# A VectorE addition between two DMAs of sums, one product with ones behind the out projection, and a new order at both ends

## The reference

```python
h = _layernorm(x)
mod = jax.nn.silu(time) @ mod_w + mod_b
shift, scale, gate = jnp.split(mod, 3, axis=-1)
h = h * (scale + 1.0) + shift
qkv = (h @ w_qkv).reshape(B, T, 3, H, e).transpose(2, 0, 3, 1, 4)
q, k, v = (qkv[0], qkv[1], qkv[2])
q = _apply_rope(_layernorm(q, q_norm_w), position)   # rotates the first 16 of 32
k = _apply_rope(_layernorm(k, k_norm_w), position)   # the other 16 pass unchanged
scores = jnp.einsum('bhqe,bhke->bhqk', q, k) / jnp.sqrt(jnp.asarray(e, q.dtype))
attn = jax.nn.softmax(scores, axis=-1)
o = jnp.einsum('bhqk,bhke->bhqe', attn, v)
o = o.transpose(0, 2, 1, 3).reshape(B, T, D)
return x + o @ w_out * gate
```

## Time and profile before

| | us |
|---|---|
| median of 3 runs | 1816.01 (1814.66 to 1819.8) |
| profiled execution | 1818.37 |
| its span, first to last instruction | 1816.5 |
| TensorE products busy | 1691.9 (93%) |
| VectorE busy | 1248.4 (69%) |
| ScalarE busy | 1024.5 (56%) |
| GpSimd busy | 721.3 (40%) |

### The profile page before, as it was taken

One profiled execution on the slowest core, in us unless ns is written; L12 is line 12 of the kernel. 1 busy time (PEld: TensorE's weight loads), 2 busy tenths in 40 slices (PEclk: granted clock), 3 DMA queues, 4 the chain that ended last, 5 costly groups with the idle time before them and its releaser, 6 DMA issues.

```text
span 1816.5 us, 32141 instructions
## 1 busy us (share of the span) xinstructions
PE 1691.9 (93%) x12326; PEld 987.8 (54%) x12326; DVE 1248.4 (69%) x1595; ACT 1024.5 (56%) x1544; POOL 721.3 (40%) x708
## 2 busy tenths in 40 slices
PE   5878899999999999999999999999999999998777
PEld 3544455555555555555555555555555555554334
DVE  8666666777777676767777776767777676765443
ACT  3335655655565566556555655665566556655442
POOL 2533244344334434443443444344434434443121
PEclk9879999999999999999999999999999999999888
DMA  6024354545545454655555464555545554544454
GB/s 216 13 47 99 83 133 105 126 107 128 117 105 135 111 132 96 134 117 107 126 119 126 99 137 108 112 121 125 125 102 131 113 115 111 128 99 96 108 116 116
DMA packets 55446, 206.43 MB, mean 114 GB/s; under 512 B 6640, under 2 KB 6640, under 8 KB 38912
## 3 DMA queue, kind: packets, MB, share of 16 engines
q0 software_dynamic: 18432, 134.23, 38.7%
q1 hardware_dynamic: 36864, 70.14, 11.3%
HBM read 53.25 MB, written 16.88 MB: 39 GB/s over the span
## 4 chain that ended last, share of the span: by engine, by line
PE 67%; DVE 21%; issue 6%; ACT 4%; DMA 2%; SPq 0%; POOL 0%; DVEq 0%; ACTq 0%; POOLq 0%
PE SA L393 10%; PE Y L320 10%; DVE cst L954 8%; PE Y L307 8%; PE MB L421 7%; PE O L412 7%; PE SM L363 6%; PE Y L310 6%; PE Y L314 6%; DVE qk_lo L943 4%; ACT probs L716 4%; DVE xin L921 3%; PE SA L397 3%; DVE bn L876 2%; PE SA L297 1%
## 5 line engine op out<-in xcount | busy, mean ns | idle before, releaser
L954 DVE TENSOR_REDUCE cst<-SM 128x2 fp32r<-128x1024 f32 x256 | 313.5, 1225 | 329.1 <-PE MB L363 329.1
L1174 POOL DMA_DIRECT2D probs<-probs x128 | 111.6, 872 | 777.6 <-ACT probs L718 748.8
L716 ACT ACTIVATE probs<-SM 128x1024 f32<-128x1024 f32 x256 | 262.0, 1023 | 260.4 <-PE SM L397 257.8
L954 DVE TENSOR_REDUCE cst<-MB 128x2 fp32r<-128x1024 f32 x256 | 311.4, 1216 | 0.0
L412 PE MATMUL O<-probs,vals 128*32 128x512 f32 x2048 | 277.1, 614 | 0.0
L718 ACT ACTIVATE probs<-SA 128x1024 f32<-128x1024 f32 x256 | 261.0, 1019 | 0.0
L623 ACT ACTIVATE rows<-Y 128x512 f32<-128x512 f32 x123 | 73.5, 598 | 281.5 <-PE Y L314 281.5
L307 PE MATMUL Y<-wqkv_hi,hT_hi 128*128 128x512 f32 x724 | 218.3, 424 | 2.8 <-ACT hT_hi L592 2.8
L310 PE MATMUL Y<-wqkv_hi,hT_lo 128*128 128x512 f32 x724 | 197.8, 396 | 6.2 <-DVE hT_lo L937 6.2
L363 PEld LDWEIGHTS SM<-qk_hi 32*128 32x128 f32 x512 | 50.0, 184 | 270.5 <-issue 80.0
L314 PE MATMUL Y<-wqkv_lo,hT_hi 128*128 128x512 f32 x724 | 195.9, 393 | 0.0
(11 more groups left out here) (197 smaller groups left out, 3466.2 us busy)
## 6 DMA issues: line engine op xcount, KB each, us to landing
probs<-probs POOLq DMA_DIRECT2D x128, 1024.0 KB, 7.7
xin<-in_x_dram SPq DMA_DIRECT2D x62, 256.0 KB, 6.9
xres<-in_x_dram SPq DMA_DIRECT2D x60, 256.0 KB, 2.6
out_dram<-xres SPq DMA_DIRECT2D x60, 256.0 KB, 3.8
shift_scale<-mod_rows SPq DMA_DIRECT2D x15, 512.0 KB, 5.9
gate<-mod_rows SPq DMA_DIRECT2D x16, 256.0 KB, 5.3
probs<-in_L_cond_w_qkv_dram SPq DMA_DIRECT2D x2, 1024.0 KB, 11.3
rows<-in_L_cond_mod_w_dram SPq DMA_DIRECT2D x2, 1024.0 KB, 11.2
```

What stands on the lines that cost most here:

```text
L716: act.activation(probs[:, a, 2:4, :], SM[:], ACT.Exp).then_inc(s_exp, 1)
L954: dve.tensor_reduce(heads[:, 2 * half:2 * half + 2, 0], bank[:], AX.X, ALU.max, negate=True).then_inc(max_out, 1)
```

## The change

**Sums over keys.** VectorE's `add_pair(s)` adds buffer 0 onto buffer 2, after the first DMA has landed and TensorE has weighed t = 2. The second DMA adds buffer 1 onto buffer 2 after that. One product with ones of buffer 2 is left; it stands in the next step behind the out projection, ahead of the third scores by key. ScalarE takes the logarithm directly from the bank, behind `guess_roots`; the copy and `add_sums` are gone. `key_exponentials(s, 0)` waits for `add_pair(s - 1)` in place of the product with ones.

**Rotation.** The second operation of `rotate` covers only the 16 rotated columns of each head. The weights of q's and k's norm for the other 16 are applied as a factor per partition (`pass_w`) in `high_qk` and `low_qk`.

**Order of VectorE.** In a step, x's statistics stand behind the maxima of t = 0, `normalize_x` at the step's end, `add_pair` ahead of the maxima of t = 3. **Order of GpSimd.** `output_low` stands ahead of the second DMA. **Order of ScalarE.** `output_high` follows the exponentials of t = 2 in every step.

**Head.** The weights of the modulation are loaded first; the statistics of the first six tiles are taken in three parts (1, 3 and 2 tiles); tiles 4 and 5 are transposed and projected earlier; the four scores by query of group 0 come after the last projection of the head. **End.** The sums of the last group are made of two products with ones that add up in one bank, without a second DMA; `project_last` is split in another way, and two of the last four additions go to GpSimd.

```diff
+            def add_pair(g):
+                dve.wait_ge(first_added, 16 * (g + 1))
+                dve.wait_ge(pv_step, TT * g + 3)
+                dve.tensor_tensor(probs[:, 2], probs[:, 2], probs[:, 0], ALU.add).then_inc(pair_added, 1)
...
             def add_keys(g, t):
                 pool.wait_ge(s_exp, 2 * (TT * g + t) + 2)
-                pool.wait_ge(pv_step, TT * g + t)
+                if t == 1:
+                    pool.wait_ge(pv_step, TT * g + t)
+                else:
+                    pool.wait_ge(pair_added, g + 1)
...
@@ tensor, scores_by_query(g, t)
-                if t == 1 and g >= 2:
-                    pe.wait_ge(sum_added, g - 1)
-                if t == 3 and g >= 1:
-                    pe.wait_ge(first_summed, g)
+                if t == 2 and g >= 2:
+                    pe.wait_ge(sum_ln, g - 1)
...
@@ tensor, step s
                 scores_by_key(s, 1)
-                if s > 0:
-                    if group(s + 1):
-                        pe.wait_ge(max_out, 2 * TT * (s + 1) + 2)
-                    add_over_keys(s - 1, 2, MB[:, 0, :])
                 weigh_values(s, 0)
...
                     project_out(n, Y[:], 4, 12)
+                if s > 0:
+                    if group(s + 1):
+                        pe.wait_ge(max_out, 2 * TT * (s + 1) + 4)
+                    add_over_keys(s - 1, MB[:, 0, :])
 
                 scores_by_key(s, 2)
...
                 scores_by_key(s, 3)
-                if group(s + 1):
-                    pe.wait_ge(max_out, 2 * TT * (s + 1) + 6)
-                add_over_keys(s, 0, MB[:, 0, :])
                 weigh_values(s, 2)
...
@@ scalar
-            def move_first_sum(g):
             def log_sums(g):
-                act.wait_ge(sum_added, g + 1)
-                act.activation(sum_inv[:], sum_inv[:], ACT.Ln).then_inc(sum_ln, 1)
+                act.wait_ge(ones_done, g + 1)
...
+                act.activation(sum_inv[:], MB[:, 0, :], ACT.Ln).then_inc(sum_ln, 1)
...
@@ vector, low_qk
-                dve.tensor_tensor(qk_lo[:, g % 2, j, :], MB[:, j, :], qk_hi[:, g % 2, j, :].bitcast(F32),
-                                  ALU.subtract).then_inc(qk_low, 1)
+                dve.scalar_tensor_tensor(qk_lo[:, g % 2, j, :], MB[:, j, :], pass_w[:, j:j + 1],
+                                         qk_hi[:, g % 2, j, :].bitcast(F32), ALU.mult, ALU.subtract
+                                         ).then_inc(qk_low, 1)
...
@@ vector, step s
-                if s > 0 and tile(s + 6):
-                    normalize_x(s + 6)
-                if s > 0 and tile(s + 7):
-                    x_statistics(s + 7)
-                    aggregate_x(s + 7)
...
                     maxima(s + 1, 0)
+                if tile(s + 7):
+                    x_statistics(s + 7)
+                    aggregate_x(s + 7)
...
+                add_pair(s)
                 if group(s + 1):
                     maxima(s + 1, 3)
+                if tile(s + 7):
+                    normalize_x(s + 7)
...
@@ gpsimd, rotate
-                pool.tensor_tensor(r, r, rope_same[:, t, j, :].unsqueeze(1).to_broadcast([P, H, E]),
-                                   ALU.mult).then_inc(rope_step, 1)
+                pool.tensor_tensor(r[:, :, 0:R], r[:, :, 0:R], rope_same[:, t, j, :].unsqueeze(1)
+                                   .to_broadcast([P, H, R]), ALU.mult).then_inc(rope_step, 1)
...
@@ tensor, behind the last step
+            pe.wait_ge(pair_added, NS)
+            pe.wait_ge(sum_ln, LAST)
+            add_last_sums(2)
             pe.wait_ge(last_low, 3)
-            for t in range(3):
-                project_last(t, 2, 3)
+            project_last(0, 0, 3)
             weigh_values(LAST, 3)
-            add_over_keys(LAST, 2, SM[:, 0, :])
-            project_last(3, 0, 3)
+            add_last_sums(1)
+            for t in range(1, TT):
+                project_last(t, 0, 3)
```

More of the change, by code:

```diff
@@ L218, in _ @@
             sp.wait_ge(bias_set, 3)
-            for j in range(3):
-                sp.dma_start(bias_rows[j][0:E, :], mod_b[j * D:(j + 1) * D].rearrange("(a n) -> a n", a=1)
-                             .to_broadcast([E, D])).then_inc(ld_modb[j], 16)
-            for n in range(TT):
-                sp.dma_start(x_rows(n), x_t[0, n]).then_inc(ld_first[n], 16)
+            for j in (1, 0):
+                load_bias(j)
+            load_first(0)
+            load_weight(0)
+            for n in range(1, TT):
+                load_first(n)
             load_weight(2)
@@ L415, in weigh_values, with add_over_keys, add_last_sums @@
                 mm.then_inc(pv_step, 1)
-            def add_over_keys(g, t, bank):
-                pe.wait_ge(first_added if t == 0 else second_added, 16 * (g + 1))
+            def add_over_keys(g, bank):
+                pe.wait_ge(second_added, 16 * (g + 1))
                 for i in range(HG):
-                    mm = pe.matmul(bank[head_rows(i), :], ones_r[:, 0:E].bitcast(F32), probs[:, t, i, :],
+                    mm = pe.matmul(bank[head_rows(i), :], ones_r[:, 0:E].bitcast(F32), probs[:, 2, i, :],
                                    start=True, stop=True, skip_group_check=True)
                 mm.then_inc(ones_done, 1)
+            def add_last_sums(a):
+                for i in range(HG):
+                    mm = pe.matmul(MB[head_rows(i), 0, :], ones_r[:, 0:E].bitcast(F32), probs[:, a, i, :],
+                                   start=(a == 2), stop=(a == 1), skip_group_check=True)
+                if a == 1:
+                    mm.then_inc(ones_done, 1)
             pe.wait_ge(consts, 5)
@@ L815, in _ @@
                     square(s + 6, 0)
-                if 0 <= s - 4 and s < LAST:
-                    output_high(s - 4)
             log_sums(LAST)
```

272 lines of the change are left out of this document (139 added, 133 removed).

## The result

| | before | after |
|---|---|---|
| median (range) | 1815.34 us (1811.9 to 1819.8, 4 runs) | 1864.87 us (1862.94 to 1868.34, 4 runs) |
| ratio, 95% interval | | 1.0274 [1.0245, 1.0302] |
| profiled execution, span | 1818.37, 1816.5 | 1868.34, 1866.5 |

A forecast was written before the change was run, and what follows sets the result against it. TensorE, 97% busy, seemed the bound, but between groups the chain runs over VectorE. Steps +1.23 us each, 53 of them +65; +3, +6.5, -5, -7 elsewhere: +62.5, giving 1878 us, range 1846 to 1918.

The forecast's parts named there:

- The step's mechanism: Middle step: the addition waits for weighing t = 2, delaying maxima and transposes; TensorE idles 1.2 us; step +1.23 us.
- K3 to Q0: Middle step, scores by key t = 3 to next group's first scores by query: 10.68 us against 10.29, +0.39.
- The products with ones: TensorE, middle step: one product removed, -0.57 us; the other moved behind the out projection, +0.88 us.
- The -0.57: Scores by key to scores by query, t = 1: without the product with ones, 3.00 falls to 2.43 us.
- The wait on GpSimd: VectorE's addition waits for the rest of a GpSimd rotation operation: 0 to 0.75 us, taken as 0.35 a step.
- +0.18: Middle step, t = 2: logarithm and inverse on ScalarE delay the exponentials and the query product by 0.18 us.
- The head: Before the steps: early statistics remove a 4.35 us wait, query products come later; -5 us, between -10 and +3.
- The ends of the loop: Steps 0 to 4 +3 us, steps 58 to 62 +6.5 us, tail from the last transposes -7 us.
- the -18: Lower bound, in us, for the ends together (-18 to +8), added to the steps' +48 to +86 for the range.
- The addition is hidden: Rival: the addition fits VectorE's 3.39 us idle time; step 25.2 us, total 1736 us; chance 0.07.
- The second DMA too late: Rival: GpSimd issues the second DMA late, delaying t = 1 exponentials; step 28.7 us, total 1938 us; chance 0.10.
- The clock falls: Rival: TensorE's stop of 1.2 to 1.9 us halves the clock every second step; +53, 1931 us; chance 0.10.

The follow-up runs named there:

- half addition: Changed kernel with VectorE's addition over 128 x 1024 instead of 128 x 2048, two of four heads not added: 1827.21 us, ratio 1.0079.
- one-product run: Kernel before without the product with ones over buffer 0 and without ScalarE's copy of its sums: 1796.29 us, ratio 0.9923.
- the wide rotation: Changed kernel with the second operation of the rotation over all 512 columns again: 1944.49 us, ratio 1.0737.
- the run with the addition and the normalising behind: Changed kernel with add_pair behind the maxima of t = 3 and normalize_x behind the next group's maxima of t = 0: 1881.26 us, ratio 1.0388.
- the ones back: Changed kernel with its one product with ones back between scores by key of t = 1 and the weighing of t = 0, logarithm between t = 1 exponentials: 1864.83 us.
- the longer addition: Changed kernel with a maximum over 128x1024 added behind VectorE's addition, values unchanged: 2048.29 us, ratio 1.1313.
- the two with the addition behind: Changed kernel with add_pair behind the maxima of t = 3: 1918.31 us; the same with normalize_x also moved behind the next maxima of t = 0: 1881.26 us.

## Why the prediction was right

**The step's mechanism: right.** The addition waits for the weighing, starts 2.34 us behind K3 (forecast 2.25), takes 2.29 (2.28), and the transposes wait for the maxima behind it. The longer and the half addition both show that it is in line there: what each added to the addition or took from it in the record (+1.65, -0.54) is what Q3 to the transposes changed by (+1.68, -0.56). K3 to Q0 without any wait on GpSimd was forecast as 10.68 and is 10.75.

**The products with ones: right in kind, one term too small.** The -0.57 was exact, also by itself in the one-product run. For the product that stands alone I took the distance of two starts, 0.88; in its new place it costs 0.99, and as much came back when it was moved away again (4.84 to 3.84). Why it costs more there was not shown; it stands between products of other kinds, where the earlier trace rows show it from one neighbour only.

**The wait on GpSimd: the size that failed.** This is the term of 0.35 with its bounds 0 and 0.75. The changed kernel has 0, because VectorE wins by 0.01 us; GpSimd waits instead, 2.15 us, off the path. Over 53 steps this is 18.6 us, about the whole error of the middle (46.9 against 65). The bounds were right: three runs in which the start moves a little show 0.37, some 0.6 and 0.90, the last against the operation of 512 columns, which the text had with its own bound of 1.28. A quantity of this kind has no typical value. It is decided by which of two starts is first, and the prediction took a mean where the value is either 0 or what is left of an operation. The shorter rotation, which the text called worth nothing, is what kept the value at 0: with the wide one the wait was 0.90 us a step.

**ScalarE: +0.03 instead of +0.18.** The logarithm started 0.13 behind K2 (939.38), not 0.2, and the inverse took 0.54 us up to the exponential at 940.55. That this term was 0.15 too large, that of the product with ones 0.11 too small and K3 to Q0 0.07 too small is luck for the sum: the three nearly cancel. So do, in part, the middle (18 us too much) and the head (6 us too little). Of the 62.5 us forecast for the span, 50.0 were measured.

**The head: wrong in sign, small.** The step that failed is the -5 us, near the wait that the row showed. That wait is gone, 0.37 us for 4.35 of the earlier trace rows. But the four query products with their maxima in line take 14.6 us from the first (88.14) to the transposes, about what the text gave them (9.6 and 4), and it then chose a value near the gain alone. TensorE of before, then of the changed kernel there:

```profile
94.19 0.49 PE L363 MATMUL SM<-qk_hi 32*128 32x512 f32 x2 [0.38 <-DVE cst L954]
...
97.59 0.73 PE L363 MATMUL SM<-qk_hi 32*128 32x512 f32 x2 [2.89 <-DVE cst L954]
```

```profile
91.11 0.49 PE L380 MATMUL SM<-qk_hi 32*128 32x512 f32 x2 [2.46 <-DVE cst L971]
...
95.28 0.79 PE L380 MATMUL SM<-qk_hi 32*128 32x512 f32 x2 [3.67 <-DVE cst L971]
...
99.39 0.80 PE L380 MATMUL SM<-qk_hi 32*128 32x512 f32 x2 [3.31 <-DVE cst L971]
...
102.74 0.72 PE L388 MATMUL SA<-ident_r,cst 128*128 128x128 f32 x4 [2.55 <-DVE cst L971]
```

Four waits for the maxima, 11.99 us together, against three of before, 6.68 us with the 3.41 of the earlier trace rows. The clock was another cost, which the prediction did not have: the mean granted clock of the head is 0.88 instead of 0.93. Up to 60 us from the start it was 1.00 in the kernel before and is 0.89 and 0.88 in the two halves of that stretch now, and from 91.9 us to the transposes it is 0.50. No run takes the head apart, so how the +1.0 divides further stays open.

**The ends of the loop: right.** +2.3, +5.7 and -5.9 against +3, +6.5 and -7.

**Two sums.** With no wait on GpSimd the prediction's steps give +47 us, where its range says +48. The bounds that it gives for the ends add up to -10.5 and +8.5; the -18 that the range starts from does not come out of them. The measured time does not depend on either.

**The rivals.** *The addition is hidden* fell with the row that was named against it: the idle time of VectorE ends with the weighing. *The second DMA too late* did not happen: it is issued at 951.51, 19.5 us behind K1, and with the median landing of 7.7 it is there 1.3 us before it is wanted; the run with the addition and the normalising behind shows that this bound is nevertheless the next one. (In one middle step of the change an exponential did wait for a DMA, 0.8 us.) *The clock falls* did not happen in the change, whose clock is 1.00 in the middle, nor with the ones back, where the stop was 1.44 us. It did happen in the four runs with stops of 1.70 us and more (the longer addition, the wide rotation and the two with the addition behind). The rival was real, for a stop 0.6 us longer than the change's.

**The exclusive lock.** The Trainium skill, SBUF — State Buffer, section Who interferes with whom, has it that a VectorE instruction with two inputs in SBUF and a GpSimd instruction that reads SBUF contend for a shared pair of ports, and that whichever issues first keeps it for the whole instruction. The rows of this case agree in both directions: 2.88 us for a GpSimd operation of 0.73 beside an addition of 2.29, and 3.19 us for that addition beside an operation of 1.28.

## What to carry to other kernels

Price a VectorE operation with two SBUF inputs together with GpSimd's schedule at its start: its cost is its own time plus 0 or the rest of GpSimd's operation, and an edit elsewhere that shifts the start by 0.2 us can turn the one into the other. Take the gain of an edit only as far as the next releaser in the same piece, and then ask what else it shifts: here 0.45 us saved on TensorE came back as 0.37 of waiting, and 0.57 as 0.38. Before lengthening a wait of TensorE, look at how long it is already, because a little more can cost the clock: here 1.44 us in every step cost nothing, and 1.70 did.

## What was not expected of the hardware

- A stop of TensorE of 1.07 us in every step left the granted clock at 1.00 for 53 steps. So did one of 1.44 us (ones back). With a stop of 1.70 us in every step it fell in 13 of 53 steps, with one of 1.97 in 21, with one of 2.75 (the longer addition) in 44. The length of a single stop does not settle it: in the run with the addition and the normalising behind, of eight stops of 2.6 to 3.0 us five were followed by a fall. A fall costs 1.3 to 1.4 us of its step (29.39 against 28.13, 29.00 against 27.65).
- The record shows an operation blocked by the other engine as busy for its whole wait: GpSimd's 0.73 us as 2.88, its 1.27 as 3.33. GpSimd's busy share rose with less work.
- Who goes first was decided by a few hundredths of a microsecond at most (0.01 in the rows shown), and in the same way in every middle step: the group of the 47 additions between 300 and 1600 us has a mean of 2293 ns in the changed kernel, that of 48 in the run with the ones back 2668 ns.

```profile
L977 DVE TENSOR_TENSOR probs<-probs 128x2048 f32<-128x2048 f32 x47 | 107.8, 2293 | 132.1 <-PE O L429 132.1
```

```profile
L978 DVE TENSOR_TENSOR probs<-probs 128x2048 f32<-128x2048 f32 x48 | 128.0, 2668 | 104.0 <-PE O L429 104.0
```
